# A graph convolution with ScalarE normalising half of group 2, adjacency's first tile ahead of x's fourth, and other first turns

## The reference

```python
h = relu(layernorm(x))                        # x [128, 128, 128] f32: graphs, nodes, features
out  = direction(h, W_fwd,  Wg_fwd,  b_fwd,  bg_fwd,  adj,   relations 2..40)
out += direction(h, W_bwd,  Wg_bwd,  b_bwd,  bg_bwd,  adj.T, relations 2..40)
out += direction(h, W_loop, Wg_loop, b_loop, bg_loop, adj.T, relation 1)
return x + relu(out)

def direction(x, W, Wg, b, bg, adj, rels):
    h = x @ W.T
    g = h @ Wg.T
    vals = (h[:, :, None, :] + b) * sigmoid(g[:, :, None, :] + bg)
    return einsum('bnmr,bmrd->bnd', adj[..., None] == rels, vals)
```

## Time and profile before

| | |
|---|---|
| median of 3 runs | 104.29 us (104.07 to 104.54) |
| the profiled execution | 104.14 us, its span 102.4 us |
| TensorE busy | 96.5 us (94%) |
| VectorE, ScalarE busy | 90.3 us each (88%) |
| GpSimd busy | 83.8 us (82%) |
| moved by DMA | 25.45 MB, 249 GB/s |
| granted TensorE clock | 0.999 of full speed |

### The profile page before, as it was taken

The page is one execution under the profiler, slowest core; times in us unless marked ns, Lnnn a source line. Parts: engine busy times, 40 slices in busy tenths (PEclk is TensorE's granted clock), DMA queues, the critical chain, the costliest instruction groups (busy, mean ns, idle before and its releaser), DMA issues.

```text
span 102.4 us, 2495 instructions
## 1 busy us (share of the span) xinstructions
PE 96.5 (94%) x802; PEld 92.5 (90%) x802; DVE 90.3 (88%) x197; ACT 90.3 (88%) x148; POOL 83.8 (82%) x158
## 2 busy tenths in 40 slices
PE   5988899999999999999999999999999999999960
PEld 2657798999999999999999999999999999999950
DVE  2289899999999999999999999999998588877661
ACT  5068889989999999999999989998999989898890
POOL 2275999999999999999999999999999999960000
PEclk9999999999999999999999999999999999999999
DMA  2899999999999999999999999999933341506345
GB/s 63 249 313 292 293 290 290 293 294 288 274 313 304 321 321 324 301 324 333 335 328 333 317 339 322 304 312 312 315 100 109 92 113 55 156 15 197 102 137 170
DMA packets 50288, 25.45 MB, mean 249 GB/s; under 512 B 866, under 2 KB 50276, under 8 KB 50276
## 3 DMA queue, kind: packets, MB, share of 16 engines
q1 hardware_dynamic: 50000, 25.17, 88.0%
q10 hardware_dynamic: 276, 0.13, 0.4%
HBM read 16.91 MB, written 8.39 MB: 247 GB/s over the span
## 4 chain that ended last, share of the span: by engine, by line
PE 80%; DMA 7%; DVE 4%; SPq 3%; ACT 3%; issue 1%
PE psum L827 25%; PE psum L805 14%; PE psum L806 14%; PE psum L810 14%; PE psum L792 13%; DMA x_all<-in_x 7%; ACT junk L467 2%; SPq L253 2%; DVE stats L554 1%; DVE xn L571 1%; DVE vals L587 1%; DVE hT_lo L597 1%; SPq L269 0%; SPq L270 0%; ACT gate L461 0%
## 5 line engine op out<-in xcount | busy, mean ns | idle before, releaser
L366 POOL TENSOR_SCALAR xn<-x_all,mean_neg,rstd 128x128 f32<-128x128 f32 x96 | 42.4, 456 | 0.5 <-issue 0.3
L805 PE MATMUL psum<-w_hi,hT_hi 128*128 128x256 f32 x128 | 34.3, 301 | 0.7 <-ACT hT_hi L427 0.3
L434 ACT ACTIVATE psum<-bias_all 128x1024 f32<-128x1024 f32 x32 | 33.0, 1032 | 0.7 <-DVE vals L587 0.6
L827 PE MATMUL psum<-vals,mask 128*128 128x128 f32 x256 | 33.6, 275 | 0.0
L806 PE MATMUL psum<-w_lo,hT_hi 128*128 128x256 f32 x128 | 31.6, 280 | 0.0
L827 PEld LDWEIGHTS psum<-vals,mask 128*128 128x128 f32 x256 | 31.1, 191 | 0.0
L554 DVE BATCH_NORM_STATS2 stats<-x_all 128x6 f32<-128x256 f32 x64 | 24.0, 420 | 3.5 <-DMA x_all<-in_x 3.5
L587 DVE TENSOR_TENSOR vals<-psum,gate 128x512 f32<-128x512 f32 (+1 forms) x33 | 21.9, 665 | 4.0 <-ACT gate L461 3.8
L805 PEld LDWEIGHTS psum<-w_hi,hT_hi 128*128 128x128 f32 x128 | 24.1, 188 | 1.5 <-issue 0.9
L348 POOL TENSOR_TENSOR rstd<-var_eps,minus_half 128x16 f32<-128x16 f32 (+2 forms) x11 | 24.5, 2224 | 0.1
L806 PEld LDWEIGHTS psum<-w_lo,hT_hi 128*128 128x128 f32 x128 | 24.2, 189 | 0.0
(11 more groups left out here) (38 smaller groups left out, 34.5 us busy)
## 6 DMA issues: line engine op xcount, KB each, us to landing
adj_all<-in_adj SPq DMA_DIRECT2D x16, 512.0 KB, 6.5
x_all<-in_x SPq DMA_DIRECT2D x15, 512.0 KB, 6.7
out<-x_all SPq DMA_DIRECT2D x14, 512.0 KB, 6.3
out<-x_all SPq DMA_DIRECT2D x3, 256.0 KB, 2.3
x_all<-in_x SPq DMA_DIRECT2D x2, 256.0 KB, 3.0
out<-x_all ACTq DMA_DIRECT2D x1, 128.0 KB, 2.5
out<-x_all SPq DMA_DIRECT2D x1, 128.0 KB, 2.6
w_raw<-in_L_gnn_W_loop SPq DMA_DIRECT2D x1, 64.0 KB, 2.4
```

The source lines that it names most:

```text
L366: last = pool.tensor_scalar(xn[:, g % XN, j * D:j * D + D], x_all[:, g * GC + j * D:g * GC + j * D + D], mean_neg[:, b % BATCH_SLOTS, k:k ...
L434: nc.scalar.activation(prod_ps[s].rearrange("p g a d -> p g (a d)"), bias_all[:, :, :].rearrange("p a d -> p (a d)").unsqueeze(1) .to_broa ...
L805: nc.tensor.matmul(to, hi, w_hi[:, :], start=False, stop=False, skip_group_check=True)
L827: last = nc.tensor.matmul(to[:, j * D:j * D + D], mask[:, g % MASKS, j * N:j * N + N], vals[:, s, j * D:j * D + D], start=True, stop=True)
```

## The change

Seven edits, all but one of order or share.

- SyncE: adjacency's tile 0 is loaded ahead of x's tile 3.
- Shares: ScalarE's group is 2 and no longer 1, and it takes only the two graphs that GpSimd doesn't (L444). GpSimd has four graphs of group 1 (was 0), two of group 2 (was 4), three of group 5 (was 4) and four of group 6 (was 2). VectorE gets one graph of group 5 and loses its two of group 6.
- GpSimd: normalise 1 stands between the coefficients of batches 1 and 2. The shift is computed for the first four rows of batch 2 instead of those of batch 1.
- ScalarE: the first turns go seed 0, relu 0, seed 1, gate 0, relu 1, edges 0, normalise, gate 1, relu 2, seed 2, relu 3, edges 1, seed 3.
- VectorE: message 0 goes ahead of low part 1, normalise 3 ahead of statistics 6, output 0 and 1 and the statistics between them move, normalise 5 comes in, normalise 6 goes out.
- `means_before` counts batches with a GpSimd share only, which gives the same counts here.
- The 64 bytes a partition of `minus_half` move behind the tiles of the coefficients, so that `mask` and the four small tiles after it start 64 bytes lower (the mask at byte 172160).

```diff
-    POOL_SHARES = (0, 0, 4, 0, 4, 4, 2)
+    POOL_SHARES = (0, 4, 2, 0, 4, 3, 4)
-    ACT_GROUP = 1
+    ACT_GROUP = 2
...
-        minus_half = sb("minus_half", [128, BATCH])
         mask = sb("mask", [128, MASKS, GROUP * N])
...
         mean_neg = sb("mean_neg", [128, BATCH_SLOTS, BATCH])
+        minus_half = sb("minus_half", [128, BATCH])
...
-            return sum(any(pool_share(g) or g == ACT_GROUP for g in ...
+            return sum(any(pool_share(g) for g in ...
...
             load_x(2)
+            load_adj(0)
             load_x(3)
-            load_adj(0)
...
-                    pool.tensor_tensor(shift[:, 0:n], mean_neg[:, s, 0:n], rstd[:, s, 0:n], ALU.mult
+                    pool.tensor_tensor(shift[:, :], mean_neg[:, s, 0:GROUP], rstd[:, s, 0:GROUP], ALU.mult
...
             coefficients(1)
+            normalise(1)
             coefficients(2)
...
-                for j in range(GROUP):
+                for j in range(pool_share(ACT_GROUP), GROUP):
...
             relu_turned(0)
+            seed(1)
+            sigmoid(0)
+            relu_turned(1)
+            edges(0)
             normalise()
-            seed(1)
-            relu_turned(1)
-            sigmoid(0)
-            edges(0)
             sigmoid(1)
             relu_turned(2)
             seed(2)
+            relu_turned(3)
             edges(1)
-            relu_turned(3)
             seed(3)
...
             row_stats(5)
+            messages(0)
+            low_part(1)
+            normalise(3)
             row_stats(6)
-            low_part(1)
-            messages(0)
-            row_stats(7)
-            normalise(3)
             messages(1)
             low_part(2)
+            row_stats(7)
             row_stats(8)
+            output(0)
             row_stats(9)
             low_part(3)
             messages(2)
-            output(0)
+            output(1)
+            normalise(5)
+            low_part(4)
             row_stats(10)
-            low_part(4)
-            output(1)
-            row_stats(11)
             messages(3)
             output(2)
-            normalise(6)
+            row_stats(11)
             low_part(5)
```

More of the change, by code:

```diff
@@ L231, in means_before @@
         def means_before(b):
-            return sum(any(pool_share(g) or g == ACT_GROUP for g in range(BATCHES[k][0], BATCHES[k][1] + 1)) for k in range(b))
+            return sum(any(pool_share(g) for g in range(BATCHES[k][0], BATCHES[k][1] + 1)) for k in range(b))
         def mask_by_act(g):
```

## The result

| | before | changed |
|---|---|---|
| median of 22 runs | 104.12 us | 103.86 us |
| the profiled execution, its span | 104.14, 102.4 us | 104.05, 102.3 us |
| TensorE busy | 96.5 us (94%) | 94.7 us (93%) |

The changed kernel takes **0.9971 of the time before, 95% interval 0.9960 to 0.9982**: 0.3% faster, a change smaller than 0.5% but clear of zero. The forecast was 104.55 us, slower than before by 0.29 us; by the medians it came out faster by 0.26 us. The range (104.0 to 104.95) does not hold the result. The forecast added its 0.29 to a median of three runs, 104.29, where 22 runs give 104.12, so 0.17 us of the 0.69 us between forecast and result is the base and not the change.

A forecast was written before the change was run, and what follows sets the result against it. TensorE, busy 94% of the span, was taken as the bound, so the start of group 7's turn counted. The three-run median 104.29 + 0.29 for GpSimd's late turn 6, masks zero, gave about 104.55 us; range 104.0 to 104.95.

The forecast's parts named there:

- Masks at another address: TensorE's sums, which read the moved masks: 0.3 us either way by comparison with the turns, taken as zero.
- GpSimd's queue sets turn 6: GpSimd's queue, with three more rows before turn 6, delays that turn to 24.30 us, against 23.91.
- The price at turn 7: TensorE's turn of group 7 starts at 27.04 us instead of 26.75, +0.29 us, and all later groups follow.
- Contention: GpSimd's two rows of group 2 beside VectorE's normalise 3: 0 to 0.2 us lost, taken as 0.06.
- rival B: Each of GpSimd's two rows of group 2 waits for VectorE rows, 0.5 us in all: 105.05 us; chance 0.09.
- The early stage: TensorE before turn 6: products 2 gain 0.10 us, turn 4 comes at 18.20; hidden by the wait at turn 6.
- Rival A: Turn 6 not held by GpSimd, so early gains of 0.10 and 0.22 us show: 103.97 us; chance 0.13.
- Rival C: GpSimd late again at turn 10, turn 10 or 14 costing 0.1 to 0.3 us more: 104.65 to 104.85; chance 0.12.

The follow-up runs named there:

- e1: Kernel before with only minus_half's 64 bytes moved behind the coefficients, so the masks start 64 bytes lower; 103.41 us against 104.53, ratio 0.9909.
- e14: The kernel of e1 measured once more, on one chip with e13 and e15; 103.43 us, 0.9871 of the kernel before.
- e2: Changed kernel with minus_half back in its old place, so the masks stand at their old address; 104.43 us against 104.53, ratio 0.9996.
- e4: Changed kernel with minus_half between masks and statistics, so only the four small tiles return to their old places; 103.56 us against 104.53, ratio 0.9912.
- e13: The changed kernel itself measured again, on one chip with e14 and e15; 103.67 us against 104.63 for the kernel before, ratio 0.9902.
- e5: Kernel before with var_eps's 256 bytes ahead of the masks, minus_half in its old place; 104.18 us against 104.20, ratio 0.9998.
- e11: Kernel of e1 with 64 empty bytes ahead of w_hi, moving the products' weights but not the identity; 104.68 us against 104.68, ratio 1.0008.
- e16: Kernel of e1 with 64 empty bytes ahead of bias_all only, the products' weights keeping their place; 103.64 us against 104.63, ratio 0.9896.
- e6: Kernel before with var_eps ahead of the masks and minus_half behind the coefficients; 103.52 us against 104.20, ratio 0.9918.
- e12: Changed kernel with one more graph of group 5 on VectorE, one row less for GpSimd; 103.19 us against 104.68 for the kernel before, ratio 0.9842.
- e15: The kernel of e12 measured once more, on one chip with e13 and e14; 103.42 us, 0.9880 of the kernel before.
- e9: Kernel of e1 with 64 empty bytes ahead of the identity, moving the products' weights too; 104.73 us against 104.68 for the kernel before, ratio 1.0011.
- e10: Kernel before with 64 empty bytes ahead of the identity, masks at their old place; 104.78 us against 104.68, ratio 1.0002.

## Why the prediction was wrong

**The step that failed is "Masks at another address ... I take zero."** It priced the address by the instructions that read the masks, the sums, against the turns, which do not. The effect was in neither. The products became faster, which touch neither the masks nor minus_half, and so the bound of 0.3 us either way was the bound of the wrong term. The address was worth 1.12 us with no other edit (e1) and 1.20 (e14). With the masks at their old place the rest of the change shows neither the gain nor the forecast loss (e2).

**GpSimd's queue sets turn 6: right, its length 0.27 us too long.** Turn 6 was forecast at 24.30 for statistics of group 1 at 5.56, 18.74 later. Measured: 18.47, held by a GpSimd row for 0.48 us, where 0.6 was forecast (e2, e4 and e13: 18.52, 18.48 and 18.58). Of the difference 0.13 lies ahead of the first row of group 1 (8.69 - 6.18 = 2.51, where 8.20 - 5.56 = 2.64 was taken) and 0.03 in seven rows (3.02 for 3.05); the rest is spread over the queue in smaller pieces.

**The price at turn 7, +0.29 us: mis-sized, it is near zero.** With the queue as measured, statistics at 5.56 give turn 7 at 5.56 + 21.27 = 26.83, 0.08 later than before: 0.27 less by the queue, and 0.06 more because from turn 6 to turn 7 it took 2.80 us and not 2.743. The other traces bear it out. From the statistics of group 1 to turn 7 there are 21.27, 21.32, 21.28 and 21.38 us in the changed orders (changed kernel, e2, e4, e13). In the eleven kernels with the old orders (before, e1, e5 to e11, e14, e16) it is 21.06 to 21.85, on average 21.43; they wait for other transfers too and scatter more. Counted from the start of the span turn 7 comes at 27.08 on average with the changed orders and at 27.01 with the old ones, within a scatter of over 1 us (26.45 to 27.53).

**And yet the rest of the change costs something once the masks stand well.** e13 less e14 is +0.24 us, by medians. In their traces it is not ahead of turn 7 (27.06 and 27.20) but behind it: 65.16 us and 64.98. With the new orders 17, 14 and 15 groups are fast (changed, e4, e13), with the old ones 18, 18, 18 and 17 (e1, e6, e14, e16). The medians' 0.24 us is small beside the scatter of the runs, and their intervals overlap. At the old address there is no such price (e2: 65.82, before: 65.81), and e2's median is not above that of before either.

**Contention (rival B): 0.08 us, where 0.06 was taken.** GpSimd's two rows of group 2 took 0.96 us beside VectorE's normalise 3; undisturbed they would take 0.88, by the seven rows in 3.02 (0.45 for the last, 0.43 for each ahead of it). In e4 it was 0.96 us too, in e2 1.01 and in e13 1.04, a loss of 0.08 to 0.16 us, inside the 0 to 0.2 of the forecast. By the Trainium skill (SBUF — State Buffer, "Who interferes with whom") a GpSimd operation that comes behind a VectorE operation in a two-port mode waits for the whole of it. These rows lost 0.04 to 0.08 us each, where one VectorE row takes 0.34, so that the full price, rival B's 0.5 us, did not come.

**The early stage: right to 0.2 us.** Turn 4 came 12.44 us after the statistics (18.62 - 6.18), where 12.64 (18.20 - 5.56) was forecast. TensorE arrived early at turn 6 and stood, so that none of this counted.

**Rival A** had a similar time for another reason. Its mechanism, turn 6 not held, is refuted by the 0.48 us of idle time. **Rival C**, a second lateness of GpSimd at turn 10, didn't come there: from turn 7 to 10 the changed kernel takes 8.18 us (27.45 to 35.63), no longer than before. It came in another form, as follows.

**A new limit.** With 2.695 us a group, four groups take 10.78 us, and GpSimd's batch takes 10.84 (coefficients at 19.32 and 30.16 in the changed kernel; the next five batches 10.82 to 10.88). The forecast had GpSimd gain 0.13 us on TensorE with every batch. It is now a little slower than TensorE, and lies closer behind it with the new shares (three more rows before turn 6). In the changed kernel the turns of groups 14 and 22, each the first of a batch, last 0.63 and 0.66 us instead of 0.60, and after each of them two groups are slow again (2.77 and 2.74, 2.80 and 2.75 us):
```profile
46.41 0.63 PE L792 MATMUL psum<-ident,xn 128*128 128x128 f32 x4
...
49.18 0.60 PE L792 MATMUL psum<-ident,xn 128*128 128x128 f32 x4
...
51.92 0.60 PE L792 MATMUL psum<-ident,xn 128*128 128x128 f32 x4
...
54.62 0.60 PE L792 MATMUL psum<-ident,xn 128*128 128x128 f32 x4
```
In all ten traces with fast groups the slow stretches behind turn 7 begin like this, with a turn, products or sums that came late by 0.01 us or more. The reverse does not hold: in group 15 of e1 and group 23 of e6 the products came 0.02 to 0.03 us late and stayed fast, and in e6 group 19 (2.77 us) and in e16 group 23 (2.79) were followed by fast groups at once. So a short hold of TensorE can put the products back to the slow rate; it was not tried by itself.

**What stays open:** why the move of the masks and minus_half, which the products don't read, and that of w_hi and w_lo, which they do, set the products' rate; whether the masks' place or that of minus_half is the one that counts; whether it is the reading of the masks by TensorE or their writing by ScalarE and GpSimd that counts; and whether residues of 128 bytes are the right grain, as only 0, 16, 64 and 80 were tried. The masks of the fast kernels (172160, 172416) are both 128 past a multiple of 256, so a grain of 256 bytes fits as well.

## What to carry to other kernels

An edit that moves a tile in memory is a change of its own, and in a kernel whose TensorE never pauses it can outweigh every change of order: give each kernel of a comparison the same addresses, or test the addresses alone first. To price such an edit, compare the start-to-start times of every kind of matmul, not only of those that read the tile. And a helper engine whose queue has no gap (GpSimd here) sets the earliest time of what it feeds: count its rows. Here one row of 0.43 us less brought the next engine's step forward by 0.30 to 0.41 us (e12, e15) and the median down by 0.25 us, with intervals that overlap.

## What the runs showed of the hardware

- Moving the 64 bytes of minus_half from ahead of the masks to behind them changed the spacing of matmuls with other operands: 128x256 products went from 0.47 to 0.45 us for four, the group from 2.743 to 2.695 us, the kernel by 0.8 to 1.3% (e1, e14, and e6 with var_eps moved as well).
- With w_hi and w_lo 64 bytes higher there was no gain and the group took 2.753 us, with the masks at 0 (e9, e11) as at 64 (e10).
- The first measurement of the changed kernel gave 0.9971 of the kernel before, a later one 0.9902 (e13), with intervals that don't meet; e4, the same but for the small tiles, gave 0.9912. The comparisons differ by more than the price of any edit here but the address; no run says why.
- Within one execution the products change between the two rates while granted clock and instructions are the same: in the changed kernel there are 1.50 us from the first product to the first sum in groups 14 and 15 and 1.45 us in groups 16 to 20, at a granted clock of 1.00.
